# Causal attention taken in pairs of heads, with the loads cut by batch entry

## What is computed

```
scores = jnp.einsum('bhqd,bhkd->bhqk', qh, kh) / math.sqrt(32)
scores = jnp.where(ki <= qi, scores, -10000.0)
attn = jax.nn.softmax(scores, axis=-1)
out = jnp.einsum('bhqk,bhkd->bhqd', attn, vh)
x = x + jnp.tanh(g_xattn[3]) * out
```

## Time and profile before

| | us |
|---|---|
| median of 3 runs (4181.95 to 4186.58) | 4185.96 |
| the profiled execution, its own time | 4189.84 |
| its span, first to last instruction | 4188.10 |
| TensorE busy | 3171.2 (76%) |
| VectorE busy | 2871.7 (69%) |
| ScalarE busy | 1891.7 (45%) |
| GpSimd busy | 743.7 (18%) |

### The profile page before, as it was taken

How to read it: one execution, slowest core, us unless ns; L and a number is a source line. 1 busy time by engine, 2 the same in 40 slices (tenths; PEclk the granted TensorE clock), 3 DMA queues, 4 the chain that set the end, 5 groups by cost and what they waited for, 6 DMA issues and landing times. The chain is left out here.

```text
span 4188.1 us, 67033 instructions
## 1 busy us (share of the span) xinstructions
PE 3171.2 (76%) x21144; PEld 1593.4 (38%) x21144; DVE 2871.7 (69%) x5255; ACT 1891.7 (45%) x2857; POOL 743.7 (18%) x611
## 2 busy tenths in 40 slices
PE   4999379988679999999952677868996217758982
PEld 2444234433345656556622333331222103224541
DVE  4222742336789999999938666247885886987877
ACT  2222122223279999999912333226773011434541
POOL 4222020001210000000040333020113201650112
PEclk9999579999799999999975788879998558978995
DMA  3000300010000000000021000102221200013201
GB/s 131 0 0 0 121 1 0 0 63 0 13 21 11 6 11 11 11 11 6 1 80 54 11 0 4 59 11 64 61 60 35 80 0 0 0 61 81 46 20 48
DMA packets 57392, 124.62 MB, mean 30 GB/s; under 512 B 12336, under 2 KB 19504, under 8 KB 55344
## 3 DMA queue, kind: packets, MB, share of 16 engines
q1 hardware_dynamic: 57264, 122.86, 9.9%
HBM read 72.37 MB, written 8.39 MB: 19 GB/s over the span
## 5 line engine op out<-in xcount | busy, mean ns | idle before, releaser
L998 DVE TENSOR_REDUCE s_top<-ps 128x1 f32<-128x512 f32 x1024 | 657.4, 684 | 35.0 <-PE ps L893 34.8
L967 ACT ACTIVATE s_prob<-ps,s_shift,m_sq 128x1024 int16<-128x1024 f32 x512 | 615.2, 1202 | 34.3 <-DVE s_shift L1006 34.2
L893 PE MATMUL ps<-s_ks,s_qs 128*128 128x512 f16 x1024 | 353.2, 387 | 64.7 <-issue 18.1
L898 PEld LDWEIGHTS ps<-ident,s_prob 128*128 128x128 f16 x4096 | 273.1, 98 | 123.7 <-DVE m_o L1016 53.1
L898 PE MATMUL ps<-ident,s_prob 128*128 128x128 f16 x4096 | 314.7, 220 | 0.7 <-ACT s_prob L967 0.5
L886 PE MATMUL ps<-s_ks,s_qs 128*128 128x512 f16 x1024 | 307.5, 382 | 0.9 <-ACT s_prob L967 0.5
L242 PE MATMUL ps<-ident,s_parts 128*128 128x128 f16 x1024 | 126.3, 300 | 225.3 <-POOL s_parts L233 223.0
L1519 PE MATMUL ps<-s_prob,s_hv 128*64 128x512 f32 x512 | 274.7, 619 | 0.2 <-ACT s_prob L1552 0.2
L973 ACT ACTIVATE s_probT<-ps 128x1024 f16<-128x1024 int16 x256 | 262.1, 1024 | 7.3 <-PE ps L898 6.9
L1552 ACT ACTIVATE s_prob<-s_prob,s_mbias,s_mscale 128x512 f32<-128x512 f32 x256 | 195.2, 806 | 96.5 <-DVE s_prob L1635 95.7
L558 DVE SCALAR_TENSOR_TENSOR s_prod<-ps,scale,s_silu 128x512 f32<-128x512 f32 x64 | 48.0, 751 | 229.9 <-ACT s_silu L542 229.9
(11 more groups left out here) (303 smaller groups left out, 6364.1 us busy)
## 6 DMA issues: line engine op xcount, KB each, us to landing
s_qs<-m_qT SPq DMA_DIRECT2D x144, 128.0 KB, 2.3
s_ks<-m_kT SPq DMA_DIRECT2D x144, 128.0 KB, 2.3
x_sb<-in_x SPq DMA_DIRECT2D x1, 4096.0 KB
s_rows<-in_ctx SPq DMA_DIRECT2D x16, 256.0 KB, 2.9
context_parts<-m_cT SPq DMA_DIRECT2D x1, 4096.0 KB, 17.2
m_nat<-in_L_ffn_W_up SPq DMA_DIRECT2D x4, 1024.0 KB, 9.5
m_nat<-in_L_ffn_W_gate SPq DMA_DIRECT2D x4, 1024.0 KB
m_nat<-in_L_ffn_W_down SPq DMA_DIRECT2D x4, 1024.0 KB
```

The lines of the kernel that those rows point to most:

```text
L893: pe.matmul(quarter_at(q), qs[:, hb, bass.ds(t * P, P)], ks[:, hb, cols(q, 512)], start=True, stop=True).then_inc(s.top_scored, 1)
L898: j = pe.transpose(turned(half, F16)[:, cols(m, P)], prob[:, u, cols(8 * half + m, P)].bitcast(F16), k.ident[:])
L967: act.activation(prob[:, u, cols(half, HALF)], pair(half).rearrange("p m n -> p (m n)"), ACT.Exp, bias=shift[:, u:u + 1], scale=sq[:, bass ...
L998: dve.tensor_reduce(top4[:, u, q:q + 1], quarter_at(q), AX.X, ALU.max).then_inc(s.top_read, 1)
```

## The change

The 64 items become 32: a pair of heads of one batch entry. Per item m = (pair, b), with `ITEMS` = 32 and all engine programs written out without a loop:

- *Loads*: per pair and batch entry, not per head: for each of 2 heads 3 parts of queries and of keys, each 32 partitions x 512 tokens: 12 DMAs. Both first pairs are loaded, all entries, before the first shift row.
- *Shift rows*: one turn of 16 columns and one copy per item; four DMAs per item, as many in all as before.
- *Scores*: as before for each head, in pieces (e = 0, 1, 2; head j), with three PSUM banks in rotation.
- *Mix*: per block of keys four fp32 products, each with 32 stationary columns and an output of its own of 32 partitions: values of head 0, values of head 1, ones, ones. The values are read from the context where it lies; `hv` and its copies are gone. The blocks of keys are mixed in three visits between scores and top scores of the neighbouring items.
- *Output*: ScalarE copies sums and numerators (64 partitions each). Once per four heads and batch entry, TensorE turns the sums with a product against a matrix `pick` of 4 columns (four fp32 products), VectorE inverts 128 x 16 numbers, TensorE turns the numerators, VectorE multiplies by gate and inverse into `y`, GpSimd adds `y` to x.

```diff
-        qs = s.sb("qs", [P, R, N], F16)
-        hv = s.sb("hv", [P, 2, T, 2 * HD], F32)
+        qs = s.sb("qs", [P, 4, N], F16)
+        ones = s.sb("ones", [P, HD], F32)
+        pick = s.sb("pick", [P, 4], F32)
...
         @s.block.sync
         def _(sp):
-            def load(head):
-                c, a, r = head // 4, head % 4, head % R
-                if head >= R:
-                    sp.wait_ge(s.scored, 3 * B * (head - R + 1))
-                for m, (lq, lk) in enumerate(((0, 0), (1, 0), (0, 1))):
-                    sp.dma_start(qs[cols(m, HD), r, :], qT[cols(a, HD), lq, c, :]).then_inc(loaded[r], 16)
-                    sp.dma_start(ks[cols(m, HD), r, :], kT[cols(a, HD), lk, c, :]).then_inc(loaded[r], 16)
+            def load(pair, b):
+                for j in range(2):
+                    head = 2 * pair + j
+                    c, a = head // 4, head % 4
+                    for m, (lq, lk) in enumerate(((0, 0), (1, 0), (0, 1))):
+                        for part, source, l in ((qs, qT, lq), (ks, kT, lk)):
+                            sp.dma_start(part[cols(m, HD), a, cols(b, S)], source[cols(a, HD), l, c, cols(b, S)]
+                                         ).then_inc(loaded[pair % 2][b], 16)
...
-            load(0)
+            for b in range(B):
+                load(0, b)
             sp.dma_start(ctx[:], k.ctx_in.rearrange("(t p) d -> p t d", p=P)).then_inc(s.ctx_loaded, 16)
-            load(1)
-            load(2)
+            for b in range(B):
+                load(1, b)
             sp.wait_ge(s.rows_cleared, 3)
-            for head in range(H):
-                for b in range(B):
-                    sp.wait_ge(s.shift_copied, B * head + b + 2)
+            for m in range(ITEMS):
+                pair, b = m // B, m % B
+                sp.wait_ge(s.shift_copied, m + 1)
+                for j in range(2):
                     for l in range(2):
-                        sp.dma_start(qs[ROWS + l:ROWS + l + 1, head % R, b * S:(b + 1) * S],
-                                     shiftT[cols(l, KT), b, :]).then_inc(shifted[b], 16)
-                if head + 3 < H:
-                    load(head + 3)
+                        sp.dma_start(qs[ROWS + l:ROWS + l + 1, 2 * (pair % 2) + j, cols(b, S)],
+                                     shiftT[cols(2 * j + l, KT), b, :]).then_inc(shifted[b], 16)
+                if m >= B and pair + 1 < PAIRS:
+                    sp.wait_ge(s.scored, 6 * (m - B + 1))
+                    load(pair + 1, b)
...
-            def mix(n, a, b):
-                pe.wait_ge(s.num_ready, n + 1)
-                for t in range(KT):
-                    j = pe.matmul(mixed_at[0:2 * HD, t * P:S], hv[:, a, b * KT + t, :],
-                                  prob[:, b % 2, START[t]:START[t] + S - t * P], start=(t == 0), stop=(t == KT - 1))
+            def mix(m, t):
+                pair, b = m // B, m % B
+                if t == 0 and m:
+                    pe.wait_ge(s.evacuated, 2 * m)
+                pe.wait_ge(s.exp_ready, 6 * m + 2 * min(t, 2) + 2)
+                for rows, of in ((0, None), (2 * HD, ones)):
+                    for j in range(2):
+                        lhsT = ctx[:, b * KT + t, cols(2 * pair + j, HD)] if of is None else ones[:]
+                        i = pe.matmul(mixed_at[rows + j * HD:rows + (j + 1) * HD, t * P:S], lhsT,
+                                      prob[:, m % 2, j, START[t]:START[t] + S - t * P], start=(t == 0), stop=(t == KT - 1))
...
+            def turn_sums(i):
+                for q in range(KT):
+                    w = pe.matmul(turned_at[:, cols(q, 4)], sums[:, b, cols(q, P)], pick[:], start=True, stop=True)
+            def turn_num(i):
+                for q in range(KT):
+                    w = pe.transpose(turned_at[:, cols(q, P)], num[:, b, cols(q, P)], k.ident32[:])
...
+            for m in range(ITEMS + 2):
+                after, ahead = m + 1 < ITEMS, m + B < ITEMS
+                if after:
+                    score(m + 1, 0, 0)
+                    score(m + 1, 0, 1)
+                if ahead:
+                    top(m + B, 0)
+                if out_of(m - 1) is not None:
+                    turn_sums(out_of(m - 1))
+                if m < ITEMS:
+                    mix(m, 0)
+                if after:
+                    score(m + 1, 1, 0)
+                    score(m + 1, 1, 1)
+                if m < ITEMS:
+                    mix(m, 1)
+                if ahead:
+                    top(m + B, 1)
+                if out_of(m - 1) is not None:
+                    turn_num(out_of(m - 1))
+                if after:
+                    score(m + 1, 2, 0)
+                    score(m + 1, 2, 1)
+                if m < ITEMS:
+                    mix(m, 2)
+                    mix(m, 3)
+                if ahead:
+                    turn_shift(m + B)
```

More of the change, by code:

```diff
@@ L2096, in attention_causal @@
         later = s.sb("later", [P, P], F16)
         laterT = s.sb("laterT", [P, P], F16)
[L2098 to L2105, removed]
+        prob = s.sb("prob", [P, 2, 2, 1280], F32)
@@ L2147, in _ @@
                                pattern=[[1, P]], channel_multiplier=-1).then_inc(s.consts_ready, 1)
[L2148 to L2169, removed]
+            pool.affine_select(out=pick[:], in_=pick[:], compare_op=ALU.not_equal, fill=1.0, base=0,
+                               pattern=[[-HD, 4]], channel_multiplier=1).then_inc(s.consts_ready, 1)
+            for i in range(OUTS):
+                c, b = i // B, i % B
+                x = k.x[:, cols(b, KT), cols(c, P)]
+                pool.wait_ge(s.weighed, i + 1)
+                pool.tensor_tensor(x, x, y[:, i % 2, :].rearrange("p (q n) -> p q n", q=KT), ALU.add).then_inc(s.added, 1)
@@ L2220, in one_head @@
[L2220 to L2238, removed]
@@ L2252, in _, with top @@
-            one_head(H - 2, 2, 96 * (H // R), True)
-            one_head(H - 1, 3, None, True, last=True)
-            pe.wait_ge(s.added, H - 1)
-            turn_output(H - 2)
-            pe.wait_ge(s.added, H)
-            turn_output(H - 1)
+            def top(m, j):
+                pair, b = m // B, m % B
+                a = 2 * (pair % 2) + j
+                n = 2 * m + j
+                if j == 0:
+                    pe.wait_ge(loaded[pair % 2][b], 192 * (pair // 2 + 1))
+                for q in TOPS:
+                    if n and q != 1:
+                        pe.wait_ge(s.top_read, 4 * (n - 1) + (1 if q == 3 else 3 if q == 0 else 4))
+                    if q == 2 and m and j == 0:
+                        pe.wait_ge(s.shift_copied, m)
+                    W = (q + 1) * P
+                    pe.matmul(top_at[q], qs[0:ROWS, a, b * S + q * P:b * S + W], ks[0:ROWS, a, b * S:b * S + W],
+                              start=True, stop=False)
+                    pe.matmul(top_at[q][:, q * P:W], k.ident[:], later[:], start=False, stop=True
+                              ).then_inc(s.top_scored, 1)
@@ new lines, in turn_shift, with score @@
+            def turn_shift(m):
+                pe.wait_ge(s.shift_ready, m + 1)
+                pe.transpose(shift_at, shift[:, m % 2, :, :, :].rearrange("p j l q -> p (j l q)"), k.ident[:]
+                             ).then_inc(s.shift_turned, 1)
+            def score(m, e, j):
+                pair, b = m // B, m % B
+                a = 2 * (pair % 2) + j
+                g = 6 * m + 2 * e + j
+                if e == j == 0:
+                    pe.wait_ge(shifted[b], 64 * (pair + 1))
+                if g >= 3:
+                    pe.wait_ge(s.exp_ready, g - 2)
+                for t in ((e,) if e < 2 else (2, 3)):
+                    at = score_at(g)[:, START[t] - START[e]:START[t] - START[e] + S - t * P]
+                    pe.matmul(at, ks[:, a, b * S + t * P:b * S + (t + 1) * P], qs[:, a, b * S + t * P:(b + 1) * S],
+                              start=True, stop=False)
+                    i = pe.matmul(at[:, 0:P], k.ident[:], laterT[:], start=False, stop=True)
+                i.then_inc(s.scored, 1)
@@ new lines, in _ @@
+            pe.wait_ge(s.consts_ready, 4)
+            pe.wait_ge(s.rows_cleared, 3)
+            for m in range(B):
+                top(m, 0)
+                top(m, 1)
+                turn_shift(m)
+            for e in range(3):
+                for j in range(2):
+                    score(0, e, j)
+            pe.wait_ge(s.ctx_loaded, 16)
+            for m in range(ITEMS + 2):
[26 more added lines that the diff above has]
+                    turn_shift(m + B)
@@ L2289, in one_head @@
-            def one_head(head, parity, first=False, last=False):
-                for b in range(B):
-                    n = B * head + b
-                    if b:
-                        numerator(n - 1, b - 1, parity, head)
-                    elif not first:
-                        numerator(n - 1, B - 1, 1 - parity, head - 1)
-                    if not last or b < B - 1:
```

(29 more changed lines are left out.)

232 lines of the change are left out of this document (96 added, 136 removed).

## The result

| us | before | changed |
|---|---|---|
| median (lowest to highest, 4 runs each, on one chip) | 4186.27 (4181.95 to 4189.05) | 4243.49 (4239.03 to 4246.68) |
| ratio, 95% interval | | 1.0137 [1.0119, 1.0154] |
| the profiled execution, its own time | 4189.84 | 4239.03 |
| its span | 4188.10 | 4237.2 |

The changed kernel is 1.4% slower; 4237 was forecast. The two profiled executions differ by 49.2 us and the stage by 50.4: it runs from SyncE's first load at 3759.4 to GpSimd's last addition, which ends at 4129.7 (before: 4079.4). So what lies outside the stage moved by about 1 us. The medians are further apart, 57.2 us: the profiled execution of the kernel before was slower than its four timed ones, that of the changed kernel the fastest of its four.

A forecast was written before the change was run, and what follows sets the result against it. SyncE's queue was taken to bound the changed stage; queue start, 24 items at 10.0 us and TensorE's last steps put its end at 4130.4 instead of 4079.4, +51 us: 4241 profiled, 4237 median, 1.2% slower, range 4198 to 4288.

The forecast's parts named there:

- The bound: SyncE's queue: 513 issues at 0.63 us, 323 us; 10.0 us per item in steady state; chance 0.60.
- The price of an issue: SyncE's queue: a copy inside SBUF occupies it about 0.59 us whatever its size, issues stand 0.63 apart.
- The rival with short issues: SyncE's queue: short SBUF copies spaced 0.47 us, all four quarters together; 4145 us, 41 less; chance 0.05.
- The start: SyncE's queue before the first shift row: two pairs' loads at 30.2 us each, context 0.6, stall 3.1; until 3823.6.
- Step 0: TensorE's first step: begins at 3831, given 11 us instead of 9.1 for the 1.2 GHz level after idling.
- The 24 items with loads: SyncE's queue, items 4 to 27: 10.0 us each, 241 us, from 3842.5 to 4083.5.
- The rest after the queue: Stage end from 4083.5: last shift rows, TensorE's steps 27 to 31, last output; ends at 4130.4.
- two at a time: TensorE's mix: two of four products overlap, 4.6 us between bounds 2.3 and 9.2; step 9.1.
- the lower bound of the working: TensorE's mix: all four products side by side, one mix per pair, 2.3 us; step 6.8.
- The other 4.5 us of the step: TensorE's step without the mix: 3.62, less 0.15 for a turn, plus 0.3 for visits and 0.75 for output turns.
- the serial case: TensorE's mix: quarters one after another, 9.2 us, step 13.7; 4375 us, 189 more; chance 0.12.
- the estimate of 3.9 for the mix: TensorE's mix by the skill's 2.38 rate: 9.2 / 2.38 = 3.9 us, step 8.4, 3 us less in the sum.

The follow-up runs named there:

- e1: The changed kernel with loads made whole per pair over all batch entries (96 of 128 KB instead of 384 of 32 KB): 4146.89 us, ratio 0.9905 to the kernel before.
- e4: The changed kernel with the same 384 small loads, those of the second head of a pair issued from ScalarE's queue: 4186.56 us.
- e3: The kernel before with only its loads cut in four by batch entry (24 DMAs per head, 384 in all): 4296.77 us.
- e9: The changed kernel, cut loads kept, with only the mix taken in one visit as in e5: 4242.39 us.
- e5: e1 with the whole mix in one visit at the end of the step, four quarters in turn per key tile: 4123.13 us.
- e6: e5 with the same sixteen mix products in another order, one quarter to its end and then the next: 4265.89 us.
- e8: e5 with the context's 4 MB load issued from ScalarE's queue instead of SyncE's: 4126.03 us, ratio 0.986 to the kernel before.

## Why the prediction was right, and where not

*The bound* was named rightly: SyncE's queue, in steady state and at the start. e1 (queue relieved, -97), e4 (same transfers, two queues, -57), e3 (cut loads alone, +111) and e9 (cheaper TensorE, nothing) leave no other.

*The price of an issue* held: 0.63 from the earlier trace rows against 0.6325 between starts. The rival with short issues fell: 32 KB cost 0.590. On this point the Trainium skill, "DMA: Bandwidth & Descriptors", Anatomy of one DMA, gives the sequencer some 50 ns of the fixed cost of a transfer on GpSimd's path; 384 loads on SyncE measured twelve times that, so the measurement decides for this queue.

*The start*: first shift row at 3823.6 forecast, 3826.55 measured. The issue behind the context load stalled for 4.86 us where the earlier trace rows had 3.67, and one load of pair 0, ahead of the context, took 1.73 (3777.76): 2.3 of the 3 us. That single loads can take longer could have been read before, where those of keys (line 2119, not among the rows) took up to 2.0 us. The first score came at 3830.18, about 3829 was named.

*Step 0* began at 3833.06 (forecast 3831) and was given 11 us; it took 6.5, to the shift turn of item 4 at 3839.53. The fall to the 1.2 GHz level was put one step too late: only the scores of item 0, just ahead of it, ran at that pace. The queue went on to item 4 at 3840.65, forecast 3842.5.

*The 24 items with loads*: 241 us forecast, 248.0 measured (3840.65 to 4088.67). The regular period is 10.12 for 10.04, 1.9 us in all; 8 of the 288 loads took 1.0 to 1.4 us instead of 0.59, which adds 4.5.

*The rest after the queue*: 47 us forecast, 41.1 measured (4088.67 to 4129.73). Here TensorE's step is on the path, and here the wrong term shows.

*The mix is the term that was mis-sized.* "I take 4.6, two at a time" was wrong; all four quarters run side by side, 2.17 us in one visit (e5), the lower bound of the working (2.3). The argument that the two passes of a product must follow one another in their quarter is true (e6), but the passes of four products come grouped: four first passes, then four second ones, so nothing is lost to it. The changed kernel's own timeline shows the pattern, here in the first block of keys of an item:

```profile
3961.21 0.62 PE L2210 MATMUL ps<-s_prob,m_ctx 128*32 128x512 f32 x2
3961.22 0.62 PE L2210 MATMUL ps<-s_prob,s_ones 128*32 128x512 f32 x2
3961.66 0.60 PE L2210 MATMUL ps<-s_prob,m_ctx 128*32 128x512 f32 x2
3961.68 0.60 PE L2210 MATMUL ps<-s_prob,s_ones 128*32 128x512 f32 x2
```

Where it waits for no shift row and runs at the 2.4 GHz level, its step is 6.54 us without output turns (3839.69 to 3846.23) and 7.92 with them (between the shift turns at 3958.25 and 3966.17), 7.2 in the mean and not 9.1. The other 4.5 us of the step were half a microsecond short for three visits (7.2 - 2.17 = 5.1) and right for one: e5 has 7.46 - 2.17 = 5.3 in steps with output turns and 6.02 - 2.17 = 3.85 in those without, 4.6 in the mean. "Against: nothing else speaks for it", said of the serial case, holds for this order of the products; in the order of e6 the mix costs 6.7 and the steps 10.6 to 12.0. The Trainium skill, "TensorE: Matmul & The Clock Gate", Part 3, reports 2.38 times for three column tiles; the estimate of 3.9 for the mix that the prediction made from it lay on the same side as its own 4.6, where e5 shows 2.17, no more than the time of one stream. Its effect on the sum was put at 3 us; six steps of 0.7 each stand on the path, which makes 4.

The total came out right because the queue hid TensorE's step, as e9 shows, and because the errors that were left nearly cancel, which is luck: begin of step 0 +2, step 0 with its hand-over -4, queue +7, the rest -6. The offset of 3.9 us from the profiled execution to the median was that of the kernel before; it had the other sign here (4239.03 against 4243.49), so that 4241 for the profiled execution was 2 us too high and 4237 for the median 6.5 too low. A forecast of e5 with the same terms would have been far off: 28 steps at 9.1 are some 65 us more than at 6.76.

*The clock*: the windows show 0.86 in the waiting stretch, for 1.00 in the earlier trace rows. Pieces of the mix run at half pace there (a first pass of 1.07 us at 3939.57, for 0.62 at 3961.21), but nearly all the time that this costs is waiting time of TensorE's anyway. A step with output turns can then last longer than the queue's period: 10.36 us from the first score at 3947.89 to the shift turn at 3958.25. The next one starts without a wait and is back in time, which is why TensorE waits in some items only and not in each, as the prediction had it. The queue's lead of four items takes this up, since it waited for no copy meanwhile; e9's clock is 0.85, and its time is the same.

## What to carry to other kernels

Count DMAs per queue, not bytes: when a load is cut finer, multiply the new number of issues by the spacing in the trace and compare it with the period of the stage; here 0.63 us each turned a gain of 1% into a loss of 1.4%, and in a strictly ordered queue small urgent copies pay for every load ahead of them. When nothing is busy in a stage, look at the queue whose waits have disappeared. In this kernel narrow fp32 products were nearly free in company, and their order decided it: give the four column quarters of the array to four independent accumulations and issue them in turn, one block of keys after another (2.17 us), rather than one quarter to its end (6.7). Before speeding up the start of a stage, find what releases its first product; in e5 it was neither the loads nor the queue but a memset of constant rows.

## What the runs showed of the hardware that was not expected

- Four fp32 products of 32 stationary columns each, issued in turn, took 2.17 us for all key blocks, no more than one stream of a quarter as many products (2.30); the same 16 in the order of the quarters cost 6.7.
- An issue on SyncE that is usually 0.59 us takes 3.7 to 5.3 behind a 4 MB load in the same queue, and, where the loads after it are of 128 KB, a few of them 1.0 to 2.8. In the changed kernel and in e9, with 32 KB loads after it, only the first was slow. With the 4 MB on ScalarE's queue this vanished (e8), but the 4 MB took 30.5 us to land instead of 15.7 (e5), and loads beside it 7.0 to 11.0 instead of 2.3.
- In long series of issues single ones take 1.0 to 1.4 us, 8 in the 288 loads of the steady stretch, with no large transfer near. Their cause stays open.
